# Hybrid attention, convolution and expert layer: low halves of the expert weights and a first fold of the values' squares on GpSimd in place of VectorE

## What is computed

```python
x = x + attn_a(layernorm(x));  x = x + ffn(layernorm(x))
x = x + attn_b(layernorm(x));  x = x + ffn(layernorm(x))

def attn_a(tokens):                       # 16 heads, DK = 16, DV = 64
    q, k, v = l2norm(q), l2norm(k), l2norm(v)      # t / max(norm(t), 1e-12), for each token and head
    sim = jnp.einsum('bhid,bhjd->bhij', q, k)
    out = jnp.einsum('bhij,bhjd->bhid', jnp.square(jax.nn.relu(sim)), v)
    out = tanh(norm(out)) * out / max(norm(out), 1e-12)
    return out_joined @ Wout

def ffn(flat):                            # 32 experts, 8 chosen for a token, and a shared one
    h = jax.nn.silu(flat @ wg.T) * (flat @ wu.T)
    acc = acc + w[:, None] * (h @ wd.T)
```

## Time and profile before

| | |
|---|---|
| time, median of 3 runs | 645.86 us (644.74 to 649.11) |
| the profiled execution's own time | 644.5 us |
| its span in the profile | 642.7 us |
| mean granted clock of TensorE | 0.945 of full speed |
| busy over the span | PE 551.9, DVE 441.1, ACT 377.7, POOL 340.4 us |

### The profile page before, as it was taken

The page is one execution under the profiler, slowest core; times in us unless marked ns, Lnnn a source line. Parts: engine busy times, 40 slices in busy tenths (PEclk is TensorE's granted clock), DMA queues, the critical chain, the costliest instruction groups (busy, mean ns, idle before and its releaser), DMA issues.

```text
span 642.7 us, 10281 instructions
## 1 busy us (share of the span) xinstructions
PE 551.9 (86%) x3336; PEld 413.2 (64%) x3336; DVE 441.1 (69%) x1059; ACT 377.7 (59%) x681; POOL 340.4 (53%) x286
## 2 busy tenths in 40 slices
PE   4487779899987887789887998999779799899996
PEld 4354546575665565568665776767667667677774
DVE  5758778786989696567577567468458458568563
ACT  5575859676776875343465744654564564565543
POOL 1634828383665642274565555554544545556564
PEclk9788989998999999889999889789799789999999
DMA  8100000000000005700471910930840661470920
GB/s 239 41 8 19 14 14 15 20 14 14 14 20 14 14 15 119 160 0 1 105 163 31 219 42 4 222 64 2 193 98 0 146 126 38 108 159 20 219 61 16
DMA packets 35205, 44.85 MB, mean 70 GB/s; under 512 B 4880, under 2 KB 18256, under 8 KB 35152
## 3 DMA queue, kind: packets, MB, share of 16 engines
q1 hardware_dynamic: 30736, 42.62, 29.6%
q10 hardware_dynamic: 4416, 1.57, 1.0%
HBM read 41.04 MB, written 3.15 MB: 69 GB/s over the span
## 4 chain that ended last, share of the span: by engine, by line
POOL 24%; issue 20%; PE 4%; DMA 1%; DVE 1%; POOLq 1%; ACT 0%; SPq 0%; DVEq 0%; ACTq 0%
POOL hl L467 20%; PE PS L1155 4%; POOL hls L471 1%; DMA wbc<-w_dram 1%; POOL fxl L431 1%; POOL rstd L424 1%; POOL mrstd L457 1%; POOLq L139 0%; DMA w_dram<-wTs 0%; DVE hb L1044 0%; DVE PS L1040 0%; POOLq L147 0%; ACT oT L682 0%; POOL ve L421 0%; POOL nmean L422 0%
## 5 line engine op out<-in xcount | busy, mean ns | idle before, releaser
L467 POOL TENSOR_TENSOR hl<-hb,hh 128x512 fp32r<-128x512 f32 x128 | 165.3, 1291 | 175.0 <-ACT hh L673 174.6
L666 ACT ACTIVATE sil<-PS 128x512 f32<-128x512 f32 (+1 forms) x136 | 81.2, 597 | 152.4 <-PE PS L1155 145.7
L1040 DVE TENSOR_TENSOR PS<-sil,PS 128x512 f32<-128x512 f32 x128 | 88.7, 693 | 113.6 <-PE PS L1155 75.8
L1155 PE MATMUL PS<-fxh,wfh 128*128 128x512 f32 x264 | 108.3, 410 | 1.9 <-issue 1.7
L1155 PE MATMUL PS<-fxl,wfh 128*128 128x512 f32 x264 | 107.6, 408 | 0.0
L1155 PE MATMUL PS<-fxh,wfl 128*128 128x512 f32 x264 | 107.5, 407 | 0.0
L1044 DVE TENSOR_TENSOR hb<-PS,wbc 128x512 f32<-128x512 f32 x128 | 88.4, 691 | 10.7 <-DMA wbc<-w_dram 6.4
L673 ACT ACTIVATE hh<-hb 128x512 fp32r<-128x512 f32 x128 | 79.8, 624 | 5.0 <-DVE hb L1044 5.0
L835 DVE SCALAR_TENSOR_TENSOR aT<-PS,rl 128x1024 f32<-128x1024 f32 x64 | 75.1, 1214 | 3.1 <-ACT rl L530 3.1
L1155 PE MATMUL PS<-hh,wfh 128*128 128x512 f32 x128 | 59.5, 465 | 16.1 <-POOL hl L467 9.6
L530 ACT ACTIVATE rl<-PS 128x1024 f32<-128x1024 f32 x64 | 62.3, 1033 | 18.4 <-PE PS L1155 18.4
(11 more groups left out here) (172 smaller groups left out, 993.7 us busy)
## 6 DMA issues: line engine op xcount, KB each, us to landing
wbc<-w_dram SPq DMA_DIRECT2D x64, 512.0 KB, 11.7
wfs<-wf_dram SPq DMA_DIRECT2D x32, 98.0 KB, 2.0
band_dram<-zero SPq DMA_DIRECT2D x16, 80.0 KB, 1.7
band<-band_dram ACTq DMA_DIRECT2D x4, 320.0 KB, 3.1
out_dram<-X SPq DMA_DIRECT2D x4, 256.0 KB, 2.3
X<-x_dram SPq DMA_DIRECT2D x1, 896.0 KB, 8.3
Osb<-wa_dram SPq DMA_DIRECT2D x1, 768.0 KB, 5.6
Osb<-wa_dram SPq DMA_DIRECT2D x1, 512.0 KB, 4.2
```

The lines of the kernel that those rows point to most:

```text
L467: g.tensor_tensor(hl[:, n % RING, :], hb[:, n % RING, :], hh[:, n % RING, :].bitcast(F32), ALU.subtract).then_inc(F("hl"), 1)
L666: s.activation(sil[0:rows, n % 2, :], PS[0:rows, G0 + n % 2, :], ACT.Silu).then_inc(F("silu"), 1)
L1040: v_.tensor_tensor(PS[:, bank, :], sil[:, n % 2, :], PS[:, bank, :], ALU.mult).then_inc(F("t"), 1)
L1155: return nc.tensor.matmul(o, w, m, start=start, stop=stop)
```

## The change

Two kinds of work go from VectorE to GpSimd. The subtractions for the low halves of the weight pieces (weight_low) are made by GpSimd, the same 32 with the same operands. And the sum of the 64 squares of a head gets a first fold on GpSimd: it adds the second 32 of a head to the first 32, in place in sqv, and VectorE then reduces 512 elements in place of 1024. A new semaphore sqh counts the folds, and value_norms waits for it in place of sqv. GpSimd's order in a batch becomes: inverse_deviation, weight_low(4b), fold of tile 0, output_norms, fold of tile 1, weight_low(4b+1), scales and values of tile 0, weight_low(4b+2), scales and values of tile 1, weight_low(4b+3).

```diff
@@ GpSimd
+            def fold_squares(n, t):
+                pool.wait_ge(A("sqv"), 2 * n + t + 1)
+                sq = sqv[:, :].rearrange("p (h m d) -> p h m d", m=2, d=DV // 2)
+                g.tensor_tensor(sq[:, :, 0, :], sq[:, :, 0, :], sq[:, :, 1, :], ALU.add).then_inc(A("sqh"), 1)
+
+            def weight_low(k):
+                pool.wait_ge(cs("wfh"), k + 1)
+                g.tensor_tensor(wfl[:, k * PC:(k + 1) * PC], wfs[:, k % 2, :], wfh[:, k * PC:(k + 1) * PC].bitcast(F32),
+                                ALU.subtract).then_inc(cs("wfl"), 1)
...
             for t in range(2):
+                fold_squares(0, t)
                 value_scales(0, t)
                 scale_values(0, t)
             for b in range(B):
                 if b + 2 < B:
                     inverse_deviation(b + 2)
+                weight_low(NG * b)
+                if b + 1 < B:
+                    fold_squares(b + 1, 0)
                 if b:
                     output_norms(b - 1)
                 if b + 1 < B:
-                    for t in range(2):
-                        value_scales(b + 1, t)
-                        scale_values(b + 1, t)
+                    fold_squares(b + 1, 1)
+                weight_low(NG * b + 1)
+                if b + 1 < B:
+                    value_scales(b + 1, 0)
+                    scale_values(b + 1, 0)
+                weight_low(NG * b + 2)
+                if b + 1 < B:
+                    value_scales(b + 1, 1)
+                    scale_values(b + 1, 1)
+                weight_low(NG * b + 3)
@@ VectorE
             def value_norms(n, t):
-                dve.wait_ge(A("sqv"), 2 * n + t + 1)
-                v_.tensor_reduce(n2[:, n % 3, t, 2 * H:3 * H], sqv[:, :].rearrange("p (h d) -> p h d", d=DV),
-                                 AX.X, ALU.add).then_inc(A("n2v"), 1)
+                dve.wait_ge(A("sqh"), 2 * n + t + 1)
+                sq = sqv[:, :].rearrange("p (h m d) -> p h m d", m=2, d=DV // 2)
+                v_.tensor_reduce(n2[:, n % 3, t, 2 * H:3 * H], sq[:, :, 0, :], AX.X, ALU.add).then_inc(A("n2v"), 1)
...
-            def weight_low(k):
-                dve.wait_ge(cs("wfh"), k + 1)
-                v_.tensor_tensor(wfl[:, k * PC:(k + 1) * PC], wfs[:, k % 2, :], wfh[:, k * PC:(k + 1) * PC].bitcast(F32),
-                                 ALU.subtract).then_inc(cs("wfl"), 1)
...
-                if b:
-                    weight_low(NG * b - 1)
                 squares(NG * b + 1)
...
-                weight_low(NG * b)
                 squares(NG * b + 2)
...
                 if more:
                     value_norms(n, 1)
                     clear_norms(n, 1)
-                weight_low(NG * b + 1)
                 squares(NG * b + 3)
...
-                weight_low(NG * b + 2)
                 squares(NG * b + 4)
...
-            weight_low(NS - 1)
```

More of the change, by code:

```diff
@@ L201, in hybrid_layer @@
         cs = Sems(ctx, nc, "id0 id half rid rbit low ind0 ind rm rf sel fpad zero sel1 sdz wah wal wfh wfl sdh sdl shz")
-        A = Sems(ctx, nc, "stats mv ve rstd xn xTh vraw sqv n2v n2q nm rr vi vc vp qkh S relu a av Oc sqO "
+        A = Sems(ctx, nc, "stats mv ve rstd xn xTh vraw sqv sqh n2v n2q nm rr vi vc vp qkh S relu a av Oc sqO "
                           "sr n th nmx rec f1 ff fhi f")
```

## The result

The changed kernel takes **676.4 us** (median of 4 runs, 673.1 to 676.9), the kernel before 647.5 us on the same chip (4 runs, 644.7 to 650.1): a ratio of 1.044 (95% interval 1.040 to 1.049), slower. The profiled execution has a span of 674.4 us, with a mean granted clock of 0.92.

The account below looks back on a forecast made before the run. The attention stage was taken as bound by a chain through VectorE, with TensorE waiting on it. Terms 27.0 - 1.3 - 5.1 + 6.7 + 2.4 + 0 - 1.0 = +28.7 us gave 673 us; own range 668 to 679, overall 658 to 685.

Parts of the forecast that it names:

- The stall of step 3: Batches 1 to 6: VectorE's step-3 squares start 9.6 us behind ScalarE's squares of tile 0; 27.0 us later in all.
- The clock: Behind TensorE's longer step-3 wait, two groups run at 1.2 GHz: 1.3 us in each of batches 2 to 6, 6.7 us.
- the terms for batches 1 to 6: Attention stage: late squares plus low clock, less step-4 subtractions and three waits; a batch lasts about 5 us more.
- The three holds: Batches 1, 5, 6: small VectorE operations no longer wait out GpSimd's multiplication into v; 3 x 1.7 = 5.1 us saved.
- Beginning: At the start, tile 1's fold stands behind tile 0's scaling, so TensorE waits longer for v: +2.4 us.
- End: Batch 7: the last low half comes sooner, TensorE is bound some 1.7 us earlier; 1.0 us taken back.
- Expert stage: The stage has no changed instruction and was costed at nothing.
- That the clock loss would be absent (1): Rival: wait without clock loss, 666 us, or 661 with a fifth of the 27 absorbed; chance 0.17.
- That a power would hold VectorE (2): Rival: a 2.9 us power holds output_factors 1.8 us in each of 6 batches, 684 us; slower fold similar; chance 0.11.
- the rule of the Trainium skill's page: VectorE instructions with two SBUF inputs contend with GpSimd instructions reading SBUF; the later is blocked for the other's whole length.
- That the second fold would not be late (3): Rival: faster, VectorE's relief counts in full, 629 us at the lowest, 636 with the path's share; chance 0.04.
- Slack that swallows the wait (4): Rival: unseen slack in the stages mostly swallows the 4.7 us of added wait, 646 to 652 us; chance 0.05.

Follow-up runs that it names:

- without the order (1): Changed kernel with GpSimd making the second fold (tile 1) ahead of output_norms: 661.6 us, ratio 1.027 to the kernel before.
- experiment 5: Changed kernel with the power of output_norms over 2 of its 32 columns, all folds and waits kept: 646.8 us, ratio 1.001 to the kernel before.
- experiment 6: Changed kernel with the power of output_norms made twice, one behind the other: 720.2 us, ratio 1.116 to the kernel before.
- Experiment 2: Changed kernel without the folds and sqh, so only the weight subtractions are on GpSimd: 634.1 us, ratio 0.984 to the kernel before; repeat 634.3 us.
- experiment 3: Changed kernel with the weight subtractions back on VectorE, so only the folds are on GpSimd: 689.6 us, ratio 1.070 to the kernel before.
- (7): Changed kernel with both folds ahead of output_norms and the weight subtractions back on VectorE: 660.4 us, ratio 1.023 to the kernel before.
- (8): Changed kernel with VectorE's second value reduction moved behind step 3's squares, addition into X and low halves: 659.4 us, ratio 1.022 to the kernel before.
- (10): Only the weight subtractions on GpSimd, and VectorE's second value reduction moved behind the output factors: 652.6 us, ratio 1.011 to the kernel before.

## Why the prediction was right, and where its sizes were off

**The stall of step 3** was forecast at 9.6 us from ScalarE's squares to VectorE's; it is 180.35 - 170.83 = 9.52. Its cause, the power between the folds, is shown from three sides: without the order (1), with a short power (5), with a double one (6), where the batch follows the wait one for one.

**The clock** was priced at 1.3 us in each of five batches; experiment 5 shows 1.21 in batch 4. That the wait brings the fall is shown by experiment 5; why the clock falls is not, and a version that kept TensorE busy through the wait was not tried.

**By batch**, the terms for batches 1 to 6 were 2.8, 5.8, 5.8, 5.8, 3.7 and 3.3; measured are 2.7, 5.6, 4.1, 5.7, 3.7 and 8.3. Two are off. In batch 3 the kernel before already had low clock of its own (0.66 in the windows view from 145 to 150 us), which the changed kernel has not: the batch lasted 29.6 us before, where batches 2 and 4 lasted 28.0, so 1.6 less is lost. From batch 6 to 7 the term was too small by 5.0. There the changed kernel has a second fall, which no step of the prediction held:

```profile
262.00:264.00 2.00, 1.89 (x10) 1.78 (x12) 2.00 (x3) 1.47 (x3) 0.00 (x0) 0.61 0.10 33
264.00:266.00 2.00, 2.00 (x12) 1.14 (x10) 1.97 (x7) 0.32 (x2) 0.00 (x0) 0.50 0.00 0
266.00:268.00 2.00, 2.00 (x16) 0.69 (x16) 0.85 (x10) 0.60 (x1) 0.00 (x0) 0.50 0.00 0
268.00:270.00 2.00, 1.91 (x28) 0.79 (x20) 0.00 (x0) 0.76 (x3) 0.00 (x0) 0.68 0.00 0
```

TensorE's attend in it took 3.68 us in place of 1.95. The run with weights only has a slow attend there too (3.57), so the stall alone does not explain it. Its repeat, the same kernel, has none: 1.95 us at 224.41, a granted clock of 1.00 from 224 to 228 us, and a batch 6 of 25.56 us in place of 27.18. So this fall comes in one execution and stays away in another; what decides it, and the rest of the 5.0 us, stays open.

**The three holds** of VectorE by the multiplication into v were to go, 5.1 us; they went. Experiment 2 shows how rough the price of 1.7 us each was: against the kernel before, its batches 1 and 5 are 4.0 and 2.1 us shorter, with TensorE's wait and low clock in the price, and its batch 6 is 0.7 longer, with the slow attend told of above (in the repeat they are 3.3 and 2.1 shorter, and batch 6 is 0.9 shorter). In the changed kernel batches 1 and 5 came out as forecast.

**Beginning:** +2.4 was forecast, +0.85 measured at the first copy (67.43 against 66.58). The values of batch 0 are ready at 35.53 as worked out, and TensorE's first attend then ran at full clock (1.95 us), where it took 3.55 before. That part is luck of the profiled execution: the double-power kernel of experiment 6, with the same instructions up to there, has its first copy at 69.73, which is +3.15. **End:** -1.0 was taken of a possible -1.7; from the last copy to the first expert product it is 1.75 less. **Expert stage:** priced at nothing, measured +2.5 in the span; its length lies between 385.5 and 396.4 us over the runs above without a changed instruction, so I count that as its scatter. The sum in the span is 0.85 + 30.1 - 1.75 + 2.5 = 31.7 us, against 28.7. That the total is only 3 us off is in part luck: errors of -1.6 (beginning), -1.6 (batch 3) and -0.75 (end) stand against +5.0 (batch 6) and +2.5 (expert stage). Two slips of rounding in the prediction change nothing: 225.28 - 221.32 is 4.0 and not 3.9, and 644.5 - 8 x 0.9 is 637 and not 636.

**The rivals.** That the clock loss would be absent (1) is refuted by the 0.50 above. That a power would hold VectorE (2), the rule of the Trainium skill's page SBUF — State Buffer, section Who interferes with whom, did not come, and the changed kernel's trace does not agree with it: VectorE's product f at 187.97, with both inputs in SBUF, took 0.19 us in the middle of the power of 2.90 us that started at 187.47, where such a product took 1.39 us under the multiplication into v (3). In the profile of the changed kernel 37 small VectorE operations in SBUF started during a power, 18 of them with two inputs there, and none took longer than 0.19 us. The rule as the prediction tells it is on instructions with two inputs in SBUF, so it does not cover the cast at 197.58, which has one. That the second fold would not be late (3) needed output_norms under 1 us; where the power took 1.02 (5), the time was still 647 us and not 629 to 636, since VectorE waits 0.85 and 1.97 us for the two folds. Slack that swallows the wait (4) is refuted by experiment 6, where the batch grows by the whole of the added wait.

## What to carry to other kernels

Work moved to an engine with room is priced at its place in that engine's order: look at what stands ahead of it there, and at what is queued behind whoever waits for it. Take such a change apart before judging it: here one half alone made the kernel 1.6% faster, and the other half alone 7% slower. And a place in the shadow of another engine's wait is a resource: work taken out of it, even behind a later step, can cost more than it took there.

## What the runs showed of the hardware

Which GpSimd operations hold VectorE. Under the multiplication into v (128x1024), small VectorE operations in SBUF were held to its end: products of 128x32 for 1.39 to 1.92 us in place of 0.19, and a clamp with one input, 128x48, for 1.80 in place of 0.19, and a subtraction of 128x196 for 2.06 in place of 0.35 (7). The reciprocal was not: 0.35 us at 198.44 in experiment 3, with v running from 198.22, as elsewhere; nor was a clamp that started 0.02 us behind v there (0.17 us). A weight subtraction on GpSimd held them to its end too: the clamp nmx took 0.33 us (187.22 in the changed kernel, with the subtraction from 186.91 to 187.51) in place of 0.17, and the cast at 180.13 took 0.51 us (8, with the subtraction from 180.01 to 180.61) in place of 0.18. Under a power none of the 37 was held.

TensorE's clock. Behind idle time of 5.19 us its next groups had a granted clock of 0.50 in the changed kernel, and doubling the wait to 11 us made nothing slower behind it than 5 us had (6). Behind 1.52 us it stayed at 1.00 (5). In between both were seen: 0.62 over 4 us behind 2.13 us (10), 1.00 behind 2.50 to 2.52 us (1, attend at 124.40, 155.64 and 186.88 in 1.95 us), and for one and the same first attend, behind 2.05 us, 1.00 in the changed kernel and 0.50 in experiment 6. So the length of the last wait alone does not say which clock follows.
